# Wider rows for a scattered table, an earlier residual load and merged mask products in an attention and mixture-of-experts kernel

## The reference

```
s1, s2 = q1 @ k1.T * scale + mask, q2 @ k2.T * scale + mask      # causal
out    = (softmax(s1) - lam * softmax(s2)) @ v                   # per head
x2     = layernorm(x + groupnorm(out) @ Wo)
e      = argmax(x2 @ router);  xs = x2 * sigmoid(max logit)
y      = layernorm(x2 + expert_e(xs) + shared(x2))               # gate/up 256 -> 2*512, silu, down 512 -> 256
```

## Time and profile before

| | us |
|---|---|
| runs (3) | 885.91, 888.58, 892.01; median 888.58 |
| the profiled execution | 890.63 |
| its span, first to last instruction | 888.9 |
| PE busy | 761.6 (86% of the span) |
| DVE, ACT, POOL busy | 464.9, 331.0, 304.3 |
| mean granted clock of PE | 0.932 |

### The profile page before, as it was taken

How to read it: one execution, slowest core, us unless ns; L and a number is a source line. 1 busy time by engine, 2 the same in 40 slices (tenths; PEclk the granted TensorE clock), 3 DMA queues, 4 the chain that set the end, 5 groups by cost and what they waited for, 6 DMA issues and landing times.

```text
span 888.9 us, 10662 instructions
## 1 busy us (share of the span) xinstructions
PE 761.6 (86%) x3590; PEld 381.9 (43%) x3590; DVE 464.9 (52%) x1036; ACT 331.0 (37%) x607; POOL 304.3 (34%) x262
## 2 busy tenths in 40 slices
PE   7187899997799989878998997899959867999994
PEld 3152234333244534523454353344226533666663
DVE  2765876751667765327767454774324421333332
ACT  2315443434564433255543334455613101222220
POOL 3038610123962121067510221211311204666653
PEclk9689999999799999987999899999969997999998
DMA  3753095002037220300731207000853102112100
GB/s 123 180 99 107 1 192 84 27 2 36 25 77 137 39 50 0 61 1 24 155 55 34 37 1 202 1 1 2 159 181 133 47 1 61 56 59 64 50 22 0
DMA packets 49333, 57.55 MB, mean 65 GB/s; under 512 B 11559, under 2 KB 43053, under 8 KB 47424
## 3 DMA queue, kind: packets, MB, share of 16 engines
q1 hardware_dynamic: 43024, 49.37, 25.0%
q0 software_dynamic: 3824, 6.32, 2.4%
q10 hardware_dynamic: 2432, 1.18, 0.5%
HBM read 42.67 MB, written 16.99 MB: 67 GB/s over the span
## 4 chain that ended last, share of the span: by engine, by line
PE 65%; DVE 10%; POOL 8%; DMA 7%; issue 6%; ACT 2%; SPq 0%; POOLq 0%; DVEq 0%; ACTq 0%
PE pv_ps L957 14%; PE wide_ps L1035 9%; PE s_ps L796 7%; PE wide_ps L943 7%; DVE mneg L1389 4%; PE wide_ps L783 4%; PE wide_ps L927 4%; DMA work<-x_in 3%; PE s_ps L797 3%; PE wide_ps L899 3%; PE pv_ps L1054 2%; PE misc L1054 2%; DMA slot_tokens<-tokens,slot 2%; PE misc L874 2%; PE s_ps L828 2%
## 5 line engine op out<-in xcount | busy, mean ns | idle before, releaser
L1389 DVE TENSOR_REDUCE mneg<-s_ps 128x1 f32<-128x384 f32 (+3 forms) x352 | 217.0, 638 | 105.2 <-PE s_ps L797 101.1
L1169 ACT ACTIVATE w_exp<-wide_ps 128x512 f32<-128x512 f32 x320 | 180.2, 599 | 118.9 <-PE wide_ps L943 117.6
L957 PE MATMUL pv_ps<-w_exp,work 128*64 128x512 f32 x640 | 182.3, 650 | 20.6 <-POOL w_exp L1302 18.6
L796 PE MATMUL s_ps<-w_exp 96*128 96x256 bf16 (+3 forms) x512 | 138.8, 313 | 33.5 <-DMA w_exp<-q_parts 18.3
L1302 POOL TENSOR_SCALAR_AFFINE_SELECT w_exp<-w_exp 128x1024 f32<-128x1024 f32 x64 | 70.7, 1105 | 280.7 <-ACT w_exp L1169 280.7
L943 PE MATMUL wide_ps<-w_exp 98*128 98x512 bf16 x320 | 124.0, 397 | 16.3 <-ACT w_exp L1169 15.0
L797 PE MATMUL s_ps<-mask,identb 128*128 128x128 bf16 x512 | 101.9, 227 | 0.0
L943 PEld LDWEIGHTS wide_ps<-w_exp 98*128 98x128 bf16 x320 | 31.8, 103 | 159.4 <-ACT w_exp L1169 101.3
L1035 PE MATMUL wide_ps<-w_exp,tables 128*128 x184 | 84.9, 605 | 0.0
L796 PEld LDWEIGHTS s_ps<-w_exp 96*128 96x128 bf16 x512 | 51.4, 101 | 70.9 <-DVE mneg L1389 38.8
L797 PEld LDWEIGHTS s_ps<-mask,identb 128*128 128x128 bf16 x512 | 52.3, 102 | 29.1 <-issue 5.9
(11 more groups left out here) (162 smaller groups left out, 1002.8 us busy)
## 6 DMA issues: line engine op xcount, KB each, us to landing
w_exp<-q_parts SPq DMA_DIRECT2D x96, 128.0 KB, 5.3
w_exp<-w_up_in SPq DMA_DIRECT2D x8, 1024.0 KB, 9.4
work<-x_in SPq DMA_DIRECT2D x8, 512.0 KB, 7.8
w_exp<-w_down_in SPq DMA_DIRECT2D x8, 512.0 KB, 11.5
q_parts<-w_exp SPq DMA_DIRECT2D x6, 512.0 KB, 7.0
w_exp<-k_parts SPq DMA_DIRECT2D x18, 128.0 KB, 4.0
gated_rows<-work SPq DMA_DIRECT2D x4, 512.0 KB, 3.1
x2s_rows<-x SPq DMA_DIRECT2D x4, 512.0 KB, 4.9
```

The lines of the kernel that those rows point to most:

```text
L796: nc.tensor.matmul(o, q_stack[0:KROWS, qt, hs, :], keys[0:KROWS, gs, 0:qt + 1, :], start=True, stop=False)
L957: last = nc.tensor.matmul(pv_ps[s * 64:(s + 1) * 64, :], vo[:, kt, g, :], probs[:, n % NP, s, :], start=(kt == 0), stop=(kt == qt))
L1169: nc.scalar.activation(probs[:, n % NP, s], st_bank(v), ACT.Exp, scale=float(DH) ** -0.5).then_inc(st_done, 1)
L1389: nc.vector.tensor_reduce(out=mneg[:, qt, rows[0]:rows[-1] + 1], in_=s_ps[:, (v - 1) % 2, 0:len(rows) * w].rearrange("p (r k) -> p r k", r ...
```

## The change

There are three edits.

1. The table `slot_tokens` gets rows of 64 equal numbers (256 bytes instead of 4). DVE copies the batch's token numbers 64-fold into `tokens_wide` in the task `top`; POOL scatters rows of it. The first column alone is read back. The fill is now one DMA of ACT's queue from a memset stretch of `x2` (19 times 2 KB for each of 128 partitions, 4.98 MB), issued right after ACT's last store of the start; the DMA from `spare_d` (75.5 KB, SP's queue) is gone. New waits: ACT on the memset of POOL, DVE (`top`) on the scatters of the batch before and (`x2` of the last batch) on the fill, POOL (`ids`) on the fill and on the copy.
2. In the last body SP issues the residual's load ahead of the loads of experts 2 and 3. The other bodies keep their order.
3. `score_bank` does the mask with one product for the whole bank: four heads at 128 columns each, or two, in one instruction of 512 or 256 columns. The products of all heads of a bank now form one accumulation group, started by the first.

```diff
@@ load order of the last body (SP)
                 if post:
                     store_gated(b - 1)
+                if not prep:
+                    load_residual(b)
                 if prep:
                     max_rows(b + 1, 1, turned_maxima(b, 1, -1))
                 else:
                     sp.wait_ge(st_full, st_at(b, LAST_ST[1], 1))
                     load_experts(2, 3)
                     sp.wait_ge(st_full, st_at(b, LAST_ST[2], 1))
                     load_experts(3, 4)
-                load_residual(b)
                 if prep:
+                    load_residual(b)
                     max_rows(b + 1, 2, turned_maxima(b, 2, -1))
@@ table read (SP)
-                sp.dma_start(rows_of[:, i:i + 1], slot_tokens[bass.ds(at * P, P), :]).then_inc(ids_loaded[g], 16)
+                sp.dma_start(rows_of[:, i:i + 1], slot_tokens[bass.ds(at * P, P), 0:1], allow_slow_non_contiguous=True).then_inc(ids_loaded[g], 16)
@@ score_bank (PE)
+                o = s_ps[:, (v - 1) % 2, 0:len(rows) * w].rearrange("p (n k) -> p n k", k=w)
                 for n, hs in enumerate(rows):
-                    gs = hs // 4
-                    o = s_ps[:, (v - 1) % 2, n * w:(n + 1) * w]
-                    nc.tensor.matmul(o, q_stack[0:KROWS, qt, hs, :], keys[0:KROWS, gs, 0:qt + 1, :], start=True, stop=False)
-                    last = nc.tensor.matmul(o[:, w - P:w], identb[:], mask[:], start=False, stop=True)
+                    nc.tensor.matmul(o[:, n], q_stack[0:KROWS, qt, hs, :], keys[0:KROWS, hs // 4, 0:qt + 1, :], start=(n == 0), stop=False)
+                last = nc.tensor.matmul(o[:, :, w - P:w], identb[:], mask[:].unsqueeze(1).to_broadcast([P, len(rows), P]), start=False, stop=True)
                 last.then_inc(bank_full, 1)
@@ fill (ACT; the memset is POOL's)
+            act.wait_ge(none_set, 1)
+            act.dma_start(slot_tokens.rearrange("(p n c) o -> p n (c o)", p=P, n=FILLS),
+                          none_yet.unsqueeze(1).to_broadcast([P, FILLS, E * COPIES])).then_inc(none_filled, 16)
@@ ids (POOL)
-                    pool.wait_ge(tokens_ready, 32)
+                    pool.wait_ge(tokens_spread, b + 1)
+                    pool.wait_ge(none_filled, 16)
                     nc.gpsimd.indirect_dma_start(out=slot_tokens, out_offset=bass.IndirectOffsetOnAxis(ap=slot[:, t:t + 1], axis=0),
-                                                 in_=tokens[:, t:t + 1], in_offset=None).then_inc(tokens_scattered, 16)
+                                                 in_=tokens_wide[:, arg], in_offset=None).then_inc(tokens_scattered, 16)
@@ top (DVE)
+                    dve.wait_ge(tokens_ready, 16)
+                    if b > 0:
+                        dve.wait_ge(tokens_scattered, b * QT * 16)
+                    nc.vector.tensor_copy(tokens_wide[:], tokens[:, b * QT:(b + 1) * QT].unsqueeze(2).to_broadcast([P, QT, COPIES])).then_inc(tokens_spread, 1)
```

More of the change, by code:

```diff
@@ L51 @@
 NROUTE = NTOK + E - 1
+COPIES = 64
+FILLS = 19
+assert FILLS * E >= E * NTOK + NROUTE
 WUP = DC * 2 * F
@@ L251, in build @@
 def build(nc, x, wqk, wv, wo, lams, gnw, gnb, cos_d, sin_d, ident_d, mask_d,
-          router, w_up, w_down, s_up, s_down, counts_d, tokens_d, spare_d, out):
+          router, w_up, w_down, s_up, s_down, counts_d, tokens_d, out):
     q_parts = nc.dram_tensor("q_parts", (B, 3, QT, 2, DH // 2, 16, 2, P), BF16, kind="Internal").ap()
@@ L259, in build @@
     x2s_rows = nc.dram_tensor("x2s_rows", (B, T, D), F32, kind="Internal").ap()
-    slot_tokens = nc.dram_tensor("slot_tokens", ((E * NTOK + NROUTE) * P, 1), I32, kind="Internal").ap()
+    slot_tokens = nc.dram_tensor("slot_tokens", ((FILLS * E) * P, COPIES), I32, kind="Internal").ap()
     ctx = ExitStack()
@@ L407, in build @@
         tokens = sb("tokens", [P, NTOK], I32)
+        tokens_wide = sb("tokens_wide", [P, QT, COPIES], I32)
+        none_yet = x2[:, (B - 1) * QT:(B - 1) * QT + 2].rearrange("p n d -> p (n d)").bitcast(I32)
         rows_of = sb("rows_of", [P, NROUTE], I32)
@@ L493, in build @@
         tokens_ready = sem("tokens_ready")
+        none_set = sem("none_set")
+        none_filled = sem("none_filled")
+        tokens_spread = sem("tokens_spread")
         tokens_scattered = sem("tokens_scattered")
@@ L604, in load_rest @@
                 sp.dma_start(tokens[:], tokens_d).then_inc(tokens_ready, 16)
-                sp.dma_start(slot_tokens, spare_d).then_inc(tokens_ready, 16)
             def load_q(b, qt, parts=(0, 1, 2)):
@@ L1316, in _ @@
             pool.wait_ge(ones_ready, 1)
+            nc.gpsimd.memset(none_yet, NTOK * P).then_inc(none_set, 1)
             pool.wait_ge(consts_loaded, NCONST * 16)
@@ L1457, in task @@
                     dve.wait_ge(y_rstd, b * QT + arg + 1)
+                    if b == B - 1 and arg == 0:
+                        dve.wait_ge(none_filled, 16)
                     nc.vector.tensor_scalar(x2[:, b * QT + arg], y[:, arg % 2], mv[:, arg % 2, 0:1],
@@ L1654 @@
         "tokens_d": (np.arange(NTOK)[None, :] * P + i[:, None]).astype(np.int32),
-        "spare_d": (NTOK * P + np.arange((E * NTOK + NROUTE) * P))[:, None].astype(np.int32),
         "counts_d": np.concatenate([np.arange(E), np.arange(E) - E, np.arange(NTOK) * P, np.arange(NROUTE),
@@ L1663 @@
           t["cos_d"], t["sin_d"], t["ident_d"], t["mask_d"],
-          t["router"], t["w_up"], t["w_down"], t["s_up"], t["s_down"], t["counts_d"], t["tokens_d"], t["spare_d"], out)
+          t["router"], t["w_up"], t["w_down"], t["s_up"], t["s_down"], t["counts_d"], t["tokens_d"], out)
     r = run(nc, [{n + "_in": v for n, v in arrays.items()}], core_ids=[0])
```

## The result

Four runs of the changed kernel had a median of 861.42 us (858.89 to 863.50), four of the kernel before beside them 887.34 (885.91 to 892.01). The ratio is 0.968, 95% interval 0.9645 to 0.9711: about 28 us less by the ratio and 25.9 by the medians, where 21.5 were forecast. On the 888.58 shown ahead of the forecast the ratio makes 860, just under the forecast's range of 861 to 873. The profiled execution took 861.43 (span 859.7, mean granted clock 0.951), against 890.63: 29.2 less. This is the difference that is taken apart here. Since the time of an execution moves by some 3 us either way with the granted clock of the bodies, distances inside one profile tell more than times from its start.

A forecast was written before the change was run, and what follows sets the result against it. Two waits of PE, for the residual's load and the last scatter, were taken to bound the kernel. 13.5 + 8.1 + 0.3 - 0.4 - 0 = 21.5 us took the median 888.6 to 867.1 (profiled execution 869.1); range 861 to 873.

The forecast's parts named there:

- The residual's idle and its slow clock: Ahead of and behind the last `weigh`: PE's 10.66 us idle and the slow clock go, 13.5 us gained, bounds 10.7 to 15.
- rival (c): At the start: the fill goes ahead of SP's loads at 148 GB/s, tile 2's queries 29 us late, 896; chance 0.02.
- Rival (e): Residual misses 640.1 beside batch 2's scatters and the experts: 874, or no gain there, 881; chance 0.05, half each.
- The scatter: Last scatter of token numbers: lands in 2.4 us instead of 17.94, net gain 8.1 us, bounds 0 to 10.2.
- PE idles some 3.8 us: Ahead of tile 2: PE is done by about 732.7 and waits for the gather landing at 736.5.
- I count the slow clock after the new idle stretch as well: Up products behind the new wait for tile 2: PE at slow clock, price 2.1 us.
- Copy, mask, fill: DVE's copy costs 0.4 us, merged mask products gain 0.3, the fill at the start costs 0 (bounds 0 and 4).
- The mask's 0.3: L797's mask products, 160 of 512 removed: only instruction starts saved, 0 to 0.8 us, taken as 0.3.
- (b): First body: the fill makes tile 2's queries or tile 1's maxima 4 to 8 us late, 871 to 875; chance 0.08.
- (d): Mask row at face value: 36 us gained, 831; a smaller share, 6 us, would give 861; chance 0.05.
- (a): The last scatter stays slow, by the skill's rule or a per-row cost: only 13.5 us won, 875; chance 0.07.
- (f): PE's clock does not fall in the new idle stretch, earlier slow-clock term larger: 863 to 865, within the forecast's 0.73.

The follow-up runs named there:

- residual alone: The kernel before with only the residual's load moved ahead of experts 2 and 3: 871.34 us, ratio 0.977 to the kernel before.
- wide rows alone: The kernel before with only the table of 64-number rows (wide scatter, fill, copy), residual and mask as before: 859.62 us, ratio 0.965.
- merged mask alone: The kernel before with only the mask products merged: 886.00 us, ratio 0.996.
- tile 2 early: The changed kernel with 16-byte rows, x of tile 2 gathered before the last-store wait, tile 0's owner read before the last-shared-row wait: 856.02 us, ratio 0.961.

## Why the forecast was too small, point by point

**The residual's idle and its slow clock: right in size, and half of the cause missed.** 13.5 us forecast, 13.7 measured (664.39 against 650.65 for the second group of late products), with the bias addition at 636.91 (forecast 637) and the triangle directly behind the exponentials. The residual alone shows that the new place suffices. But I took 21.74 us for what two loads of 1.5 MB ahead cost, and used the 148 GB/s in rival (c) as a rate that just happens. With wide rows the same load behind the same two takes 11.39, so about half of it was the 4-byte scatters' doing. Rival (e) names these scatters, as a risk to the moved load only; the gain of the scatter was counted at the end of TAIL alone, where it stands in the chain. The wide rows alone win nearly all of this term too.

**The scatter: right in kind, the stretch behind it mis-sized.** The landing was forecast at 2.4 and came out at about 2.1 (3.20 - 1.05), PE was next bound by the shared expert as forecast, and the table read of 4 bytes from 256 cost nothing (median to landing 1.9, 2.0 before). The step that failed is "PE idles some 3.8 us" with its companion, "I count the slow clock after the new idle stretch as well": net 8.1 forecast, 12.6 measured. From the last row added to tile 2 I had 736.5 - 726.64 = 9.9 us, and 2.1 for the clock; it took 7.5. Of the 4.5 us, 0.9 is the issue of the gather behind the store (5.8 forecast, 714.92 - 709.98 = 4.94 measured), 1.5 its landing (4.0 forecast, 2.48 measured) and 2.1 the clock, which did not fall; there was no idle stretch either. PE's own work up to there had also been put too short: 6.1 us behind the last row (732.7 - 726.64), where it took some 7.4, mostly since tile 0 is transposed only 1.07 us behind that row. So of the 3.8 idle one part was work, and the quicker gather took the rest. The 4.0 was the row of a gather that POOL issued right behind another and behind the first table read the earlier trace rows. It takes 3.8 to 4.0 wherever the scatter is slow (4.01 with the residual alone, 3.90 and 3.83 with rows of 4 and 8 bytes); for the gather behind the store a free-standing one was the nearer case. The median landing of the 23 gathers of the kernel before is 2.8 us, and that row was not used.

**A gain that I had not counted: the clock in TAIL, 2.9 us net of the copy.** These are windows of the kernel before:

```profile
685.00:690.00 5.00, 5.00 (x17) 3.91 (x15) 0.42 (x1) 0.37 (x1) 0.00 (x0) 0.66 0.00 0
...
700.00:705.00 5.00, 3.95 (x15) 1.86 (x14) 2.48 (x11) 0.58 (x2) 0.00 (x0) 0.80 0.30 105
```

and this is one of the changed kernel, whose eight windows from 670 to 710 us all have 1.00:

```profile
675.00:680.00 5.00, 4.08 (x21) 3.65 (x22) 1.67 (x7) 0.37 (x1) 0.64 (x1) 1.00 0.00 0
```

From the first projection of TAIL to the last shared row the kernel before takes 49.0 us, the merged mask alone 49.0, the kernel without merging 48.9, the wide rows alone 47.7, the last one (tile 2 early) 48.9, and all the others 46.0 to 46.1. I had not looked at the clock there. The first drop starts some 8 to 10 us behind the first projection, the second some 15 later. At first I took them for a late effect of the residual's idle stretch, which three of these five kernels have (the wide rows alone only 0.88 us of it, and one drop). The other two refute that. The kernel without merging has no such stretch and the same two drops, and so has the last kernel; two of its windows:

```profile
668.00:673.00 5.00, 3.89 (x15) 2.87 (x13) 1.89 (x7) 0.00 (x0) 0.20 (x1) 0.80 0.00 0
...
683.00:688.00 5.00, 5.00 (x17) 2.33 (x18) 2.50 (x13) 0.80 (x2) 0.00 (x0) 0.66 0.20 70
```

Up to 702 us that kernel issues the same instructions as the one with rows of 16 bytes, which has no drop. So the drops differ between executions of the same work, and up to 2.9 of the 29.2 us are this pair of profiles and not the change; the medians of the four runs each lie 25.9 apart. What decides whether the clock falls there stays open.

**Copy, mask, fill: as forecast.** The copy of TAIL took 0.29 us (forecast 0.4). The mask's 0.3 cannot be seen: PE is at the last `weigh` 0.2 us later, not earlier; by the bank of four heads it was rather 1 to 2. The fill landed 18.5 us after its issue at 41.23 and PE waited 18.6 us for the queries instead of 18.3, so rivals (b) and (c) did not happen.

**The rivals.** (e) fell with the bias addition at 636.91, (d) with the bank of four heads, which got 0.03 us shorter and not 0.7, and with PE no earlier at the last `weigh`. (a) fell with the table read at 3.20. The Trainium skill (page "DMA: Bandwidth & Descriptors", section "Specifications") puts line rate at 512 B and says that the engine does a read-modify-write below. As a rule on the size of a write the runs do not bear it out for latency: scatters of 256-byte rows, 64-byte rows and lone 4-byte numbers all reach the table read in 3.2 us. A read-modify-write of a block that several writes share would fit the halving, but no run here shows the mechanism. (f) came closest: no idle stretch ahead of tile 2, and the clock stayed up; its 863 to 865 lacked the shorter gather and TAIL's clock. The forecast for the profiled execution was 869.1, it is 861.4: 4.5 of the 7.7 are the tile phase, 3.3 TAIL (2.9 in place of -0.4, and perhaps no gain of the change), and the other terms cancel.

## What to carry to other kernels

A slow small DMA has two prices: its own landing on the chain, and what it takes from every transfer that runs beside it; before two changes to neighbouring queues are given a term each, ask whether one of them removes both waits. A table that is scattered into needs its entries apart: here a pitch of 64 bytes gets all of it, whatever is written there. And when a stretch is priced after a change, look at the granted clock along the whole of it, and use the row of a transfer in the same company as the one that is forecast.

## What was not expected of the hardware

- Scatters of 128 entries: the last of four lands after 17.8 to 18.4 us at a pitch of 4 bytes, 9.2 at 8, 4.0 to 4.2 at 16 and about 2.1 at 64 and 256; at 16 and 256 it makes no difference whether the entry is filled.
- Some 8 to 18 us behind the first of four scatters at a pitch of 4 bytes, the loads of SP's queue move at 88 to 123 GB/s with a DMA share of 0.84 to 1.33; with the wide rows 320 to 389 GB/s at 0.86 to 1.05. From 5 to 10 us behind it the rate is 180, 241, 303 and 404 GB/s at pitches of 4, 8, 16 and 64 bytes.
- A second large DMA issued on ACT's queue behind a first of the same size held ACT for 9.72 us; the first took 0.93.
- The granted clock of PE falls to between 0.66 and 0.80 in one window of TAIL in five of the fourteen profiles (in four of them again some 15 us later) and not in the others, with the same work on PE there.
